# Unread products of identity by identity put into TensorE's stream at section starts, fills and drains of a four-layer attention and FFN kernel

## The reference

```python
x = x + attention(ln(x), ctx)              # L0a: 16 heads of 16, softmax
x = x + fake_quant_ffn(ln(x))              # L0f: 704 hidden, weights and inputs rounded to 8 bits
x = x + pruned_attention(ln(x), ctx)       # L1a: weights stored turned; keeps 90% of the key columns
x = x + bitlinear_ffn(ln(x))               # L1f: 1024 hidden, ternary weights
x = x + attention(ln(x), ctx, mask)        # L2a: weights stored turned; masked keys
x = x + lora_experts(ln(x))                # L2f
x = x + gated_memory_attention(ln(x), ctx) # L3a
x = x + expert_mixed_attention(ln(x))      # L3g: gates from pooled tokens; L3f: attention with mixed weights
```

## Time and profile before

| what | value |
|---|---|
| median of 3 runs | 1405.55 us (1405.08 to 1406.5) |
| profiled execution: time, span | 1407.29 us, 1405.2 us |
| mean granted clock of TensorE | 0.875 |
| busy: PE, DVE, ACT, POOL | 1074.4, 952.5, 814.0, 299.8 us |

### The profile page before, as it was taken

The page is one execution under the profiler, slowest core; times in us unless marked ns, Lnnn a source line. Parts: engine busy times, 40 slices in busy tenths (PEclk is TensorE's granted clock), DMA queues, the critical chain, the costliest instruction groups (busy, mean ns, idle before and its releaser), DMA issues. The chain is left out here.

```text
span 1405.2 us, 28372 instructions
## 1 busy us (share of the span) xinstructions
PE 1074.4 (76%) x9341; PEld 882.5 (63%) x9346; DVE 952.5 (68%) x2563; ACT 814.0 (58%) x2846; POOL 299.8 (21%) x358
## 2 busy tenths in 40 slices
PE   3999946578888724557999969999978764767774
PEld 2788733357777612444787759999967663655563
DVE  3688877736777667784777746666568855777772
ACT  1777756747777626774776652121133214998984
POOL 1233200012222101001222200000011203667661
PEclk7899979559999956776999989999998865899998
DMA  6231000000000000003221000000000000000001
GB/s 206 67 109 45 9 0 0 0 12 15 14 11 12 2 0 1 0 0 90 74 74 49 9 1 0 0 0 0 1 23 15 22 1 1 1 1 0 0 1 61
DMA packets 44421, 32.59 MB, mean 23 GB/s; under 512 B 16184, under 2 KB 43456, under 8 KB 44352
## 3 DMA queue, kind: packets, MB, share of 16 engines
q1 hardware_dynamic: 44352, 31.72, 7.6%
HBM read 23.32 MB, written 2.10 MB: 18 GB/s over the span
## 5 line engine op out<-in xcount | busy, mean ns | idle before, releaser
L687 ACT ACTIVATE L1a_pr<-L1a_scores,L1a_nm 128x128 f32<-128x128 f32 x256 | 93.5, 418 | 5.5 <-DVE L1a_nm L743 4.8
L687 ACT ACTIVATE L2a_pr<-L2a_scores,L2a_nm 128x128 f32<-128x128 f32 x256 | 90.3, 381 | 5.8 <-DVE L2a_nm L743 5.8
L687 ACT ACTIVATE L3f_pr<-L3f_scores,L3f_nm 128x128 f32<-128x128 f32 x256 | 91.8, 392 | 2.2 <-DVE L3f_nm L743 2.2
L687 ACT ACTIVATE L0a_pr<-L0a_scores,L0a_nm 128x128 f32<-128x128 f32 x256 | 90.3, 381 | 4.1 <-DVE L0a_nm L743 4.1
L502 POOL TENSOR_TENSOR L3f_mix<-L3f_mix,L3f_mixed_more 128x516 f32<-128x516 f32 (+1 forms) x32 | 68.8, 2170 | 69.2 <-DVE L3f_mixed_more L820 69.2
L687 ACT ACTIVATION_READ_ACCUMULATOR L1a_pr<-L1a_scores,L1a_nm 128x1 f32 x256 | 65.6, 256 | 0.0
L1857 POOL TENSOR_TENSOR x_all<-x_all,L3a_xn 128x256 f32 (+1 forms) x16 | 12.6, 811 | 231.7 <-DVE L3a_xn L1881 231.7
L1598 ACT COPY L2f_xTb<-L2f_xT 128x256 f32<-128x256 f32 x16 | 6.4, 406 | 93.3 <-PE L2f_inner L1524 93.3
L1535 PE MATMUL L2f_inner<-L2f_taT,L2f_loraBT 128*128 128x128 f32 x512 | 59.6, 275 | 0.0
L687 ACT ACTIVATION_READ_ACCUMULATOR L3f_pr<-L3f_scores,L3f_nm 128x1 f32 x256 | 59.2, 231 | 0.0
L1524 PEld LDWEIGHTS L2f_inner<-L2f_xTb,L2f_wiT 128*128 128x128 f32 x512 | 58.6, 193 | 0.4
(11 more groups left out here) (523 smaller groups left out, 3321.3 us busy)
## 6 DMA issues: line engine op xcount, KB each, us to landing
setup_ctx_nat<-in_ctx SPq DMA_DIRECT2D x4, 512.0 KB, 5.5
x_all<-in_x SPq DMA_DIRECT2D x1, 2048.0 KB, 12.4
L0a_ctxT<-ctxT_all SPq DMA_DIRECT2D x16, 128.0 KB, 2.0
L_ffn_w<-in_L_ffn_w SPq DMA_DIRECT2D x2, 1024.0 KB, 6.2
L1a_ctxT<-ctxT_all SPq DMA_DIRECT2D x16, 128.0 KB, 2.0
L2a_ctxT<-ctxT_all SPq DMA_DIRECT2D x16, 128.0 KB, 2.0
L3a_mem<-in_ctx SPq DMA_DIRECT2D x16, 128.0 KB, 2.0
out<-x_all SPq DMA_DIRECT2D x1, 2048.0 KB, 7.5
```

What stands on the lines that cost most here:

```text
L687: ex = act.activation(pr[q.s][:, j, h, :], S[j][:, h * P:h * P + P], ACT.Exp, bias=nm[q.s][:, j, h:h + 1], scale=-1.0, accum_out=ls[q.s][: ...
```

## The change

A new helper `stay_busy` issues n products of a bf16 identity (`g.identb`, 128x128) by itself, read four times over (512 columns), into a bank; nothing waits for them and nobody reads the result. It is called in six kinds of place, on TensorE only: 18 products ahead of the first transpose in L0a and L3f; in L1a and L2a 3 behind each of the four groups of weight transposes and 4 more ahead of the first transpose of the input; in the two filling steps 2 behind every piece; in the draining steps 3 behind every piece, 5 behind `turn_recips`; 32 at the start of L0f; 18 at the start of L3g. `T[0]` and `S[0]` are the banks of the transposed probabilities and of the scores. L2f and L3a pass an empty function and stay as they are.

```diff
--- before.py
+++ after.py
@@ -90,6 +90,12 @@
 
 
 
+def stay_busy(pe, g, bank, n):
+
+    for _ in range(n):
+        pe.matmul(bank[:, :], g.identb[:, :], g.identb[:, :].unsqueeze(1).to_broadcast([P, 4, P]), start=True, stop=True)
+
+
 class Turned:
 
 
@@ -98,7 +104,7 @@
         self.banks, self.lots = banks, lots
         self.ps, self.sb = sec.sem("turned_ps"), sec.sem("turned_sb")
 
-    def tensor(self, pe, ident):
+    def tensor(self, pe, ident, between):
         for n, (sources, _) in enumerate(self.lots):
             if n >= 2:
                 pe.wait_ge(self.sb, n - 1)
@@ -106,6 +112,7 @@
                 rows, cols = src.shape[0], src.shape[1]
                 mm = pe.transpose(self.banks[n % 2][0:cols, m * P:m * P + rows], src, ident[0:rows, 0:rows])
             mm.then_inc(self.ps, 1)
+            between()
 
     def scalar(self, act):
         for n, (sources, dst) in enumerate(self.lots):
@@ -511,9 +518,10 @@
             def _(pe):
                 arrived(pe, g, *needs)
                 if turn_w:
-                    turn_w.tensor(pe, g.ident)
+                    turn_w.tensor(pe, g.ident, lambda: stay_busy(pe, g, T[0], 3))
                     turn_w.wait(pe)
                 pe.wait_ge(s_set, SETS)
+                stay_busy(pe, g, T[0], 4 if turn_w else 18)
 
                 def turn_x(q):
                     pe.wait_ge(ln.s_xn[q.s], q.v)
@@ -636,9 +644,15 @@
                 def step(st):
                     cur, prev, nxt, new, last = st.at(0), st.at(-1), st.at(1), st.at(2), st.at(-LAG)
 
+                    filling, draining = not cur and (nxt or new), not cur and not nxt and not new
+
                     def piece(q, work, *args):
                         if q:
                             work(q, *args)
+                            if filling:
+                                stay_busy(pe, g, T[0], 2)
+                            if draining:
+                                stay_busy(pe, g, S[0], 5 if work is turn_recips else 3)
 
                     if pruned:
                         piece(cur, scores)
@@ -962,6 +976,7 @@
             with sec.block() as block:
                 @block.tensor
                 def _(pe):
+                    stay_busy(pe, g, banks[7], 32)
                     for k, (sources, _) in enumerate(lots):
                         if k % PL == 0:
                             pe.wait_ge(s_w2, k // PL + 1)
@@ -1513,7 +1528,7 @@
             @block.tensor
             def _(pe):
                 arrived(pe, g, "L2_ffn")
-                turn_w.tensor(pe, g.ident)
+                turn_w.tensor(pe, g.ident, lambda: None)
                 turn_w.wait(pe)
 
                 def first(q, s):
@@ -1956,6 +1971,7 @@
             def _(pe):
                 arrived(pe, g, "L3_ffn")
 
+                stay_busy(pe, g, bank[1][0], 18)
                 pe.wait_ge(s_mr, 2)
                 pe.matmul(bank[0][0][:, 0:NB], g.onesP[:, :], mr[:, :], start=True, stop=True)
                 for b in range(NB):
```

## The result

The changed kernel takes 1408.91 us (median of 20 runs, 1408.01 to 1411.23) against 1407.18 us for the one before (20 runs, 1405.08 to 1408.29). The ratio is 1.0016, 95% interval 1.0009 to 1.0023. The forecast was 1401.4 us, its range ended at 1405.6.

The account below looks back on a forecast made before the run. TensorE at half clock (1.2 GHz) was taken to bound section starts where it stands on the path. Terms -2.2 - 4.3 - 2.0 - 1.5 + 1.6 + 4.3 = -4.1 us gave 1401.4 us, own range 1398 to 1404, eight in ten 1396.3 to 1405.6.

Parts of the forecast that it names:

- L0a's start: L0a's block, fill and first step: transpose 2.9 us late, 2.8 and 2.3 given back, sum -2.2 us.
- L2a's: L2a's start: delay +1.6 us, fill -2.8, masks -0.8, sum -2.0 us.
- L0f: 32 products in L0f's 12.0 us wait for the scaled weights: 0 us (-0.5 to +0.5).
- the drains' products: Last tile's pieces: 0.65 us each in L0a, L2a and L3f, 2.3 in L1a, sum +4.3 us.
- the case of 1417: L1a, L2a: transposes don't count as busy, so fills stay at 1.2 GHz; kernel 1417 us, 2 of 100, within rival 3.
- L1a's first step: L1a's step behind the fill: 11.9 us against ScalarE's chain of some 9.3, so 2.6 us gained, within L1a's -4.3.
- a clock that falls between the pairs of a fill: Sign in the filling steps that would show the forecast wrong; no size given.
- L3f: L3f's block and fill: transpose 2.9 us late, pairs +0.5, first steps -1.8, sum +1.6 us (0 to +4).
- the return of 1.8 in the first steps: L3f: clock expected to rise before tile 0's step and not at 1204.24 as before, -1.8 us.
- L3g: Block of 18 before L3g's pooling: pooling 1.7 us late, 3.2 saved at the upper clock, sum -1.5 us.
- Rival 1: Drains and delays eat the gain: ScalarE binds the first steps, which shrink by half as much; 1404.8 us, 25 of 100.
- Rival 3's first case: Clock rises 6 us into every block, none before L3f's second tile: +2.9, 1408.5 us; rival 3 has 9 of 100.

Follow-up runs that it names:

- held first step: Changed kernel plus eight unread products in tile 0's step in L0a, L1a and L2a (2 behind the input transpose, 6 behind the key projection): ratio 0.9998 to the kernel before.
- L3a held: Kernel before plus 12 unread products in each step of L3a, ahead of the transposes where TensorE waits for VectorE: ratio 0.9988.
- sum of parts: Kernel before plus L0a, L1a, L2a fills with tile 0's step held, and products in L3f's steady steps and L3a's wait; none in drains: 1393.24 us.
- sum and L1f: The sum of parts plus 24 unread products in each step of L1f that has a finished pair: 1392.2 us, ratio 0.9894 to the kernel before.
- L3f as before: Changed kernel with no block of 18, no pairs and no drain products in L3f: ratio 0.9988 to the kernel before.
- kernel without drains: Changed kernel without the products in the draining steps, all else as changed: ratio 0.9969 to the kernel before.
- the block of 7: Changed kernel with 7 products in place of 18 ahead of L3f's first transpose: ratio 0.9987 to the kernel before.

## Why the prediction was wrong

Right were the prices and most of the mechanism. A product costs 0.42 us at 0.50 and 0.22 at 1.00; L0a's start (-2.1 for -2.2, in part luck, since the same code differs by up to 1.7 us there), L2a's (-2.6 for -2.0), L0f (0) and the drains' products (4.1 for 4.3, against the same kernel without them) came as worked out. The clock was up at 293.72 us, before L1a's first transpose at 296.16, and on through the fills of L1a and L2a, so the case of 1417, in which the weight transposes don't help the products behind them, did not come. Whether the transposes counted for it or the products among them alone is not told apart by a run.

Three terms failed, by 2.6, 3.1 and 1.5 us; the drains came out 1.5 better than forecast, since L3f's lost a fall of the clock that it had before.

- **L1a's first step**, taken at 2.6 us, gave 0.45 in the profile and 1.3 in four other traces. The step of the sum was "the step behind it is 11.9 (305.69 to 317.63) against ScalarE's own chain of some 9.3". That chain is right: with the clock held the step is 9.58. What I left out is that the clock that a fill has raised falls again in the step behind it, in TensorE's waits of 0.46 and 1.66 us for ScalarE. The held first step shows it. The prediction named "a clock that falls between the pairs of a fill" as what would prove it wrong; it fell one step later. In the four other traces L1a's start as a whole gave 3.6 us of the 4.3; in three of them L1f and L2f are together 1.8 us longer than before.
- **L3f**, +1.6, was +4.7 ahead of its drain. The delay of the transpose is 3.8 us and not 2.9 (the clock rises only near the block's end, 6.92 us for 18), and the return of 1.8 in the first steps turned into a loss of 0.5: again the clock was down, from 1194.8 to 1205.1. And 1.8 was too much in any case: in the three traces with the clock up at the first step's end (L3a held, sum of parts, sum and L1f) that step has 12.43 to 12.47 us and not 13.75, but the first two together 24.95 to 25.12 against 25.66, some 0.6 less. The other 2.1 us are two further falls in the steady steps, which no term had. L3f as before gives 3.9 us back at once.
- **L3g**, -1.5, was 0: the block took 7.0 us, not 6.0, and the clock was up for 2.5 us of the pooling, not 4.3. Each of these 2.5 us gave 1.0 back and not the 0.75 of the forecast, which took the 0.57 of one section start for the ratio. Taking the block away changes nothing.

The drains were sized right, so they were the largest loss that could be known beforehand: their 4.1 us of products and L3f's 4.7 took back what the starts had gained (6.4 in the profile). Rival 1 (half of the step's gain) had the right place, though for another reason than ScalarE's chain, and its 1404.8 lacked the terms of L3f. Rival 3's first case came to 1408.5, next to the 1408.91 measured, and that is half luck: its late rise is there in L3g and L3f (5.95 and 5.85 us into the block), but not in L0a, where it came after 3.4; and its terms miss by 0.7 to 2.0 us each, which partly cancels.

Where the losses in L3f's steady steps come from is shown in part. In L3a the clock falls every 13.6 to 13.7 us, once in each step of two pairs, and its last fall but one comes 7.7 us before L3g's start in all ten traces with that code, though L3g starts anywhere from 1135.07 to 1143.66. Windows of the kernel without drains, where it starts at 1135.07:

```profile
1123.95:1127.36 3.41, 0.44 (x2) 0.20 (x2) 3.27 (x12) 1.01 (x3) 0.00 (x0) 1.00 0.00 0
1127.36:1130.77 3.41, 3.16 (x9) 2.63 (x10) 3.38 (x6) 0.82 (x4) 0.00 (x0) 0.50 0.00 0
```

So L3a's steps fall in with the clock's changes, and L3f then begins in the same place towards them every time: with its code as before and that L3a, its two falls come 126.4 to 126.5 and 177.6 to 177.7 us behind its start in four traces. What moves L3f's steps (the block of 18, the block of 7, a shorter L3a) puts other steps under a fall, some 0.7 to 1 us each. Holding the clock in the steps removes them. That L3a's steps take their length from the clock's changes is the reading of these places, not the outcome of a run. Open is why the same code in L0a and L1a runs more than one way (in L1a 24.65 and 26.48 us to the scores of tile 1), and how much of the 6.6 us of the drains is such luck; single profiles don't tell.

## What to carry to other kernels

A raised clock is worth something only where TensorE stands on the path and only as long as it stays up: fill the waits of the step that follows as well, and look at the busy time of the other engines first (L3a gained 5.3 us, L1f nothing, with the clock up in both). Unread products belong in waits that they fit into at the lower speed: in a drain, whose pieces follow one another by way of other engines, each product ahead of a piece is delay, and it pays back only where the clock would have fallen. And a gain at one place can change where the clock falls in a section far behind it, so such a change is measured as a whole. Take more than one profile of the kernel before, too: a start that differs by 1.7 us between two traces of the same code can't show a gain of 2.

## What was not expected of the hardware

The same block of 18 products takes 5.70 us in L0a, where the clock rises 3.4 us into it (6.08 to 6.62 in the other traces), and 6.92 and 6.97 us in L3f and L3g, where it rises only near its end. And a loop that lets the clock fall once in each step seems to take on the clock's rhythm: L3a kept its place to the falls within 0.1 us over starts that lay 8.6 us apart.
